# Causal linear attention and soft mixture on Trainium2: gamma times v summed on VectorE and carried by two passes with ones, and a new order in the last group

## The reference, cut to what matters

```python
# x: (4, 2048, 256)
h = lambda x, W1, b1: gelu(x @ W1 + b1)
q, k, v = (h(x, W1, b1) @ W2 + b2 for each of q, k, v)
scores = einsum('bid,bjd->bij', q, k) / sqrt(256 * 512)
out = einsum('bij,bjd->bid', scores * tril, v)           # no softmax
x = layernorm(x + (layernorm(out) * ln_w + ln_b))
xn = layernorm(x, ln_gamma, ln_beta)
logits = (unit(xn) * scale) @ unit(mu)                   # mu: 256 x 16 x 16
dispatch, combine = softmax(logits, tokens), softmax(logits, slots)
slot_in = einsum('bnd,bnes->besd', xn, dispatch)
h = gelu(slot_in @ w1 + b1);  slot_out = h @ w2 + b2
out = layernorm(x + einsum('besd,bnes->bnd', slot_out, combine))
```

## Time and profile before

| | us |
|---|---|
| median of 3 runs (lowest, highest) | 622.74 (622.67, 622.85) |
| profiled execution, its own time | 622.77 |
| its span (first to last instruction) | 621.0 |
| busy in the span: PE / PEld / DVE / ACT / POOL | 605.4 / 558.0 / 426.0 / 412.4 / 342.5 |

### The profile page before, as it was taken

One profiled execution on the slowest core, in us unless ns is written; L12 is line 12 of the kernel. 1 busy time (PEld: TensorE's weight loads), 2 busy tenths in 40 slices (PEclk: granted clock), 3 DMA queues, 4 the chain that ended last, 5 costly groups with the idle time before them and its releaser, 6 DMA issues. The chain is left out here.

```text
span 621.0 us, 12379 instructions
## 1 busy us (share of the span) xinstructions
PE 605.4 (97%) x4100; PEld 558.0 (90%) x4100; DVE 426.0 (69%) x948; ACT 412.4 (66%) x920; POOL 342.5 (55%) x359
## 2 busy tenths in 40 slices
PE   7999999999999999999999999989999999999995
PEld 5989989989999999999998999989999999988884
DVE  5377677677676776777777768897555556347876
ACT  4756767667677667776776776676766666535674
POOL 1737658568485585574855856766434433103443
PEclk9999999999999999999999999999999999999998
DMA  8301012012020210110201201020000000302444
GB/s 228 104 2 69 6 63 70 1 69 69 0 68 1 66 68 0 68 65 3 68 0 68 68 2 35 1 56 15 1 1 0 0 0 1 69 1 69 148 158 169
DMA packets 29326, 30.21 MB, mean 49 GB/s; under 512 B 5326, under 2 KB 25196, under 8 KB 29292
## 3 DMA queue, kind: packets, MB, share of 16 engines
q1 hardware_dynamic: 29280, 29.78, 15.0%
q10 hardware_dynamic: 12, 0.00, 0.0%
HBM read 21.39 MB, written 8.39 MB: 48 GB/s over the span
## 5 line engine op out<-in xcount | busy, mean ns | idle before, releaser
L488 POOL TENSOR_TENSOR h_lo<-xn_all,h_hi 128x512 fp32r<-128x512 f32 x32 | 41.4, 1294 | 126.1 <-ACT xn_all L565 126.0
L563 ACT ACTIVATE h_hi<-bank,bias_col 128x512 fp32r<-128x512 f32 x96 | 66.3, 691 | 35.2 <-PE bank L690 31.8
L1067 DVE TENSOR_TENSOR state_lo<-bank,state_hi 128x512 fp32r<-128x512 f32 x57 | 39.2, 688 | 60.9 <-ACT state_hi L604 60.9
L688 PE MATMUL bank<-xnT_hi,w_hi 128*128 128x512 f32 x188 | 76.1, 405 | 0.0
L690 PE MATMUL bank<-xnT_hi,w_lo 128*128 128x512 f32 x188 | 74.3, 395 | 0.0
L689 PE MATMUL bank<-xnT_lo,w_hi 128*128 128x512 f32 x188 | 74.3, 395 | 0.0
L1460 PE MATMUL bank<-xn_all,e_tok 128*128 128x257 f32 x256 | 66.4, 382 | 0.5 <-ACT slot_inT L1388 0.3
L1365 ACT ACTIVATE e_tok<-bank,shift,xinv 128x256 f32<-128x256 f32 x64 | 36.1, 564 | 45.0 <-PE bank L1443 24.8
L1540 DVE COPY ET_all<-bank 128x256 f32<-128x256 f32 (+1 forms) x64 | 27.0, 424 | 53.3 <-PE bank L1454 52.9
L604 ACT CAST state_hi<-bank 128x512 fp32r<-128x512 f32 x57 | 33.5, 587 | 39.2 <-PE bank L830 39.1
L1532 PE MATMUL bank<-w_sb,ET_all 128*128 128x256 f32 x256 | 55.4, 380 | 0.0
(11 more groups left out here) (192 smaller groups left out, 2080.7 us busy)
## 6 DMA issues: line engine op xcount, KB each, us to landing
x_all<-in_L_attn_x SPq DMA_DIRECT2D x16, 512.0 KB, 3.5
xn_all<-in_xT SPq DMA_DIRECT2D x15, 512.0 KB, 4.4
out<-xn_all SPq DMA_DIRECT2D x15, 512.0 KB, 3.0
w_sb<-in_L_ffn_w SPq DMA_DIRECT2D x2, 512.0 KB, 5.2
xn_all<-in_L_ffn_w SPq DMA_DIRECT2D x2, 512.0 KB, 6.2
xn_all<-in_xT SPq DMA_DIRECT2D x2, 256.0 KB, 3.6
out<-xn_all SPq DMA_DIRECT2D x2, 256.0 KB, 2.5
x_all<-in_L_attn_W2k SPq DMA_DIRECT2D x1, 258.0 KB, 4.4
```

The lines of the kernel that those rows point to most:

```text
L488: pool.tensor_tensor(h_lo[:, V_SLOT, m, :], hv[:, m, :], h_hi[:, V_SLOT, m, :].bitcast(F32), ALU.subtract).then_inc(hv_split, 1)
L563: nc.scalar.activation(h_hi[:, h_slot(j, n), m, :], ps, ACT.Gelu, bias=bias(n, m))
L688: nc.tensor.matmul(ps, w[0], xs[0], start=start, stop=False, skip_group_check=shared)
L1067: nc.vector.tensor_tensor(lo[:, :, :], state_halves, hi[:, :, :].bitcast(F32), ALU.subtract).then_inc(state_split, 1)
```

## The change

1. The gamma column times v is summed per token place (partition) on DVE: `sum_v` adds chunk after chunk into `v_sum`, which has four places for the four chunks of a group; `close_sum` hands the last one on to the next group. ACT rounds the sums in pairs (`round_vsum`), POOL subtracts for the low half (`split_vsum`). `carry` is now two passes per chunk, with ones as weights, inside the chunk that needs it, and nothing is copied between output tiles. `preload`, `mark_out`, `split_gamma`, `gam_hi` and `gam_lo` are gone.
2. `causal` is one 128x128 mask in place of four; `warm_up` runs three products of the size of `mark_out`'s two.
3. `sum_mu_squares` runs ahead of `project_v(0)` of group 0, and floor, inversion and factors move ahead with it.
4. In the last two bodies the orders of ACT, DVE and POOL are written anew.

```diff
+            v_sum = asb("v_sum", [P, GT, D])
+            vsum_hi = asb("vsum_hi", [P, GT, D], F32R)
+            vsum_lo = asb("vsum_lo", [P, GT, D], F32R)
+            ones_r = asb("ones_r", [P, P], F32R)
-            causal = asb("causal", [P, GT, P])
+            causal = asb("causal", [P, P])
...
 # POOL
+                def split_vsum(g, m):
+                    pool.wait_ge(vsum_rounded, 2 * g + m + 1)
+                    pair = slice(2 * m, 2 * m + 2)
+                    pool.tensor_tensor(vsum_lo[:, pair, :], v_sum[:, pair, :], vsum_hi[:, pair, :].bitcast(F32),
+                                       ALU.subtract).then_inc(vsum_split, 1)
                 def body(g, j, ba, attend=True, project=True, settle=True, more=True):
                     a = g - 1
                     if not project:
                         invert_norms(pool, 0, 0, minus_half[:, :])
+                        invert_z(pool, a - 1, j % 2)
+                        add_ln_b(a)
                         add_beta(pool, 1, 1)
                         invert_x1(pool, a - 1, j % 2)
                         return
+                    if attend and project:
+                        split_vsum(a, 0)
                     if project:
                         split_hv(g, 0)
                     if attend:
                         invert_o(pool, a, 0)
                     if project:
+                        if attend:
+                            split_vsum(a, 1)
                         split_hv(g, 1)
                         if more:
                             split_x(g + 1)
-                        add_ln_b(g)
-                        if not more:
+                        if not attend:
+                            invert_mu_norms()
+                        if more:
+                            add_ln_b(g)
+                        else:
                             add_beta(pool, 0, 0)
                         split_ktok(g, 0)
...
+                        if not more:
+                            split_vsum(g, 0)
+                            split_vsum(g, 1)
-                    if attend and project:
+                    if attend and project and more:
                         invert_z(pool, a, (j - 1) % 2)
-                        if more:
-                            invert_x1(pool, a, (j - 1) % 2)
+                        invert_x1(pool, a, (j - 1) % 2)
 # ACT
-                def preload(ba, i):
-                    act.wait_ge(carried, CB * ba + i - 1)
-                    act.wait_ge(z_ready, TB * ba + i + 2 - i % 2)
-                    nc.scalar.copy(out_tile(i % GT), out_tile((i - 1) % GT)).then_inc(preloaded, 1)
+                def round_vsum(g, m):
+                    act.wait_ge(v_summed, GT * g + 2 * m + 1)
+                    pair = slice(2 * m, 2 * m + 2)
+                    nc.scalar.copy(vsum_hi[:, pair, :], v_sum[:, pair, :]).then_inc(vsum_rounded, 1)
...
                         round_xnT(act, 0, 0)
+                        round_vsum(a, 0)
                         round_state(ba, i + 1, tail_hi[1])
-                        preload(ba, i + 2)
-                        nc.scalar.activation(warm[:, :], warm[:, :], ACT.Exp).then_inc(table_warm, 1)
+                        round_vsum(a, 1)
+                        apply_z(act, a - 2, ja % 2, (2, 3))
                         round_state(ba, i + 2, tail_hi[2])
                         round_masked(a)
-                        preload(ba, i + 3)
-                        apply_z(act, a - 1, (ja - 1) % 2, (0, 1))
                         round_state(ba, i + 3, tail_hi[3])
-                        apply_z(act, a - 1, (ja - 1) % 2, (2, 3))
+                        nc.scalar.activation(warm[:, :], warm[:, :], ACT.Exp).then_inc(table_warm, 1)
+                        apply_z(act, a - 1, (ja - 1) % 2, range(GT))
                         return
...
                     hidden(g, j, WK1, 0)
+                    if attend:
+                        round_vsum(a, 0)
...
                         follow(0)
+                    if attend:
+                        round_vsum(a, 1)
                     hidden(g, j, WV1, 0)
 # PE
-                def carry(a, ba, i):
-                    c = i % GT
...
-                    split3(out_tile((i + 1) % GT),
-                           (gam_hi[:, c:c + 1].to_broadcast([P, P]), gam_lo[:, c:c + 1].to_broadcast([P, P])),
-                           (v_hi[:, c, :], v_lo[:, c, :]), False, False, shared=True).then_inc(carried, 1)
+                def carry(a, c, start):
+                    pe.wait_ge(vsum_split, 2 * a + c // 2 + 1)
...
+                    nc.tensor.matmul(out_tile(c), ones_r[:, :], vsum_hi[:, c, :], start=start, stop=False,
+                                     skip_group_check=True)
+                    nc.tensor.matmul(out_tile(c), ones_r[:, :], vsum_lo[:, c, :], start=False, stop=False,
+                                     skip_group_check=True)
...
                     elif c == 0:
-                        read_state(ba, i, c, p, False)
+                        read_state(ba, i, c, p, True, False)
+                        carry(a, c, False)
                         last = attend_chunk(a, c, False, True)
                     else:
-                        attend_chunk(a, c, False, False)
-                        last = read_state(ba, i, c, p, True)
+                        attend_chunk(a, c, True, False)
+                        carry(a, c, False)
+                        last = read_state(ba, i, c, p, False, True)
                     last.then_inc(chunk_done, 1)
                     if i < TB - 1:
                         update_state(a, c, i == 0)
-                        carry(a, ba, i)
 # DVE
-                def split_gamma(g):
-                    dve.wait_ge(gam_rounded, g + 1)
-                    nc.vector.tensor_tensor(gam_lo[:, :], k_tok[:, :, D], gam_hi[:, :].bitcast(F32), ALU.subtract
-                                            ).then_inc(gam_split, 1)
+                def sum_v(g, j, c):
+                    dve.wait_ge(v_biased, 2 * g + c // 2 + 1)
...
+                    gamma = k_tok[:, c, D:D + 1]
+                    if j == 0 and c == 0:
+                        last = nc.vector.tensor_scalar(v_sum[:, 1, :], v_tok[:, 0, :], gamma, None, ALU.mult)
+                    else:
+                        last = nc.vector.scalar_tensor_tensor(out=v_sum[:, c + 1, :], in0=v_tok[:, c, :], scalar=gamma,
+                                                              in1=v_sum[:, c, :], op0=ALU.mult, op1=ALU.add)
...
                         split_masked(a)
...
+                    if attend:
+                        sum_v(a, ja, 1)
+                        sum_v(a, ja, 2)
                     split_h(g, j, WQ1, 0)
...
                         follow(0)
+                        close_sum(a, ja)
                     split_h(g, j, WQ1, 1)
...
                     bias_v(g, j, 1)
+                    if not more:
+                        for c in range(GT - 1):
+                            sum_v(g, j, c)
+                        return
                     if attend:
                         add_out(dve, a, 2)
                         add_out(dve, a, 3)
                         z_summed(dve, a, 1)
-                    split_gamma(g)
+                    sum_v(g, j, 0)
...
                     floor_norms(dve, 0, 0)
                     tail_state(1)
+                    add_out(dve, a - 1, 2)
+                    add_out(dve, a - 1, 3)
                     mask_scores(a)
-                    shift_z(dve, a - 1, 1 - p)
                     tail_state(2)
                     split_masked(a)
+                    z_summed(dve, a - 1, 1)
+                    z_statistics(a - 1, 1 - p, 1)
+                    tail_state(3)
                     split_xnT(dve, 0, 0)
-                    tail_state(3)
+                    z_deviation(dve, a - 1, 1 - p)
+                    dve.wait_ge(v_split, 2 * GROUPS)
                     scale_tokens(2, 2)
+                    shift_z(dve, a - 1, 1 - p)
```

More of the change, by code:

```diff
@@ L663, in body @@
                         follow(2)
-                        if settle:
+                        if settle and more:
                             apply_z(act, a - 1, (ja - 1) % 2, range(GT))
+                        if not more:
+                            norms(act, 0, 0, range(GT))
                         follow(3)
@@ L752, in fold_weights, with warm_up @@
                     last.then_inc(ku_done, 1)
[L754 to L759 removed]
+                def warm_up():
+                    for ps in (*out_ps, state_ps):
+                        nc.tensor.matmul(ps[:, :], ident[:, :], causal[:, :].unsqueeze(1).to_broadcast([P, GT, P]),
+                                         start=True, stop=True)
                 def project_k(g, j, t):
@@ L1188, in _ @@
                 split_weight(WV2)
+                nc.vector.tensor_copy(ones_r[:, :], ones[:, :]).then_inc(ones_rounded, 1)
                 body(0, 0, 0, attend=False)
```

(1 more changed line is left out.)

87 lines of the change are left out of this document (44 added, 43 removed).

## The result

The changed kernel takes 630.12 us (median of 4 runs, 629.85 to 631.76), the kernel before 622.80 (4 runs, 622.67 to 623.61): 1.012 times as long, 95% interval 1.0101 to 1.014. The forecast was 630.4, slower. The profiled execution took 629.85 us with a span of 628.1, 7.1 more than the one before (622.77 and 621.0). The sum is right; several of its terms are not, and their errors cancel.

The account below looks back on a forecast made before the run. PE, busy 97% of the span, was taken to bound the kernel. Terms +0.5 - 1.5 - 5.9 + 4.0 + 8.6 + 1.9 = +7.6 us on 622.77 gave 630.4 us, range 624.5 to 636.

Parts of the forecast that it names:

- The last group, +8.6: Block end: late ve_z, then 7.7 us of GpSimd work, moves the end from 414.3 to 422.9, +8.6 us.
- The clock, +1.9: Routing stage: after PE idles some 8 us it begins at the low clock, +1.9 us (0 to 2.3).
- The carry, -5.9: Carries up to the last projecting body's second chunk: two passes (0.24 us) replace three (0.34 us), -5.9 us.
- The wait at chunk 0, +4.0: Chunk 0's carry in 11 groups: PE waits 0.36 us each for the split sums, +4.0 us.
- rival 1: The sums fit in: no wait at chunk 0, DVE not held in the last group; 624.8, up to 627; chance 0.17.
- mu's norms, -1.5: Group 0: factors ready long before the scores end, so PE's wait for them goes, -1.5 us.
- The one wait named in the price: Group 0, chunk 0: a possible wait for the unit mu, giving back at most 1.5 us.
- The start, +0.5: Kernel start: smaller mask starts PE 0.7 us earlier, two more warm_up passes cost time; net +0.5 us (-0.2 to +1.0).

Follow-up runs that it names:

- k1_pool: The changed kernel with add_ln_b and add_beta moved ahead of invert_z in GpSimd's queue of the last group; 626.61 us, 1.0064 of before.
- k5_nosum: The changed kernel with the sums, their rounding and split on 2 columns instead of 256, the carry reading v_hi and v_lo; 626.5 us, 1.005 of before.
- k2_warm: The changed kernel with 30 more 512-column passes on PE behind the last pass of the last group; 629.82 us, 1.0102 of before.
- b1_carry6: The kernel before with the three passes of each carry done twice; 643.89 us, 1.0329 of before.
- k6_carry4: The changed kernel with the two passes of each carry done twice; 641.99 us, 1.0297 of before.
- b2_wide: The kernel before with the carry's weights taken from plain 128x128 tiles of ktok_hi and ktok_lo instead of one repeated gamma column; 624.82 us, 1.003 of before.
- k7_delay: The changed kernel with a pow of about 1.0 us ahead of GpSimd's split_vsum(a,0) in each group; 638.91 us, 1.0252 of before.
- k3_biasv: The changed kernel with mu_factors on DVE behind bias_v(1) of the first group instead of ahead of it; 631.49 us, 1.0138 of before.
- k10_acttail: k8_hybrid with ACT's roundings ahead of its four L188, sum 2 behind the first tail state, three warm_up products, mu_factors as in the change; 621.77 us, 0.9979 of before.
- k8_hybrid: The changed kernel with group 14's z_deviation and invert_z early, ln_b(15) in halves, two warm_up products, mu_factors behind bias_v(1); 621.30 us, 0.9967 of before.

## Why the prediction was right, point by point

- **The last group, +8.6: right, +8.1.** Its mechanism is shown by k1_pool (the place of two additions in GpSimd's queue, at least 2.65 us at the mark and 3.5 in the time) and k5_nosum (1.35 of the 1.6 for the sums held by GpSimd). `ve_z` came at 411.5; the 415.2 of the forecast, less the 3.3 us by which the last scores start earlier, are 411.9. The 7.7 us of work were 7.8. The Trainium skill, "SBUF — State Buffer", section "Who interferes with whom", says that a DVE instruction with two inputs in SBUF contends with a GpSimd instruction that reads SBUF; the traces agree: 1.52 us instead of 0.49 for a sum, 3.77 instead of 1.67 for the four L212.
- **The clock, +1.9: right, +2.2** (the rest in k2_warm against the changed kernel). That the sizes are so near is partly luck: 1.9 was half of 3.7 us, taken from the kernel's start, and the low level lasted 5.5 us into the routing stage.
- **The carry, -5.9: the size failed, -3.3.** The step "0.34 us for three passes, 0.12 each for two" priced the passes rightly (b1_carry6, k6_carry4; the sum used 0.236 for two, which with 0.24 is -5.6) and assumed that every other pass keeps its spacing. The 53 carries in "groups" give -5.3. The v projection behind them takes back 0.8, of which 0.5 is shown to go with the repeated column (b2_wide, in the kernel before); the k projection takes back 0.9, cause open; waits in the last projecting body and small differences 0.3. The 0.5 of k5_nosum doesn't come on top: most of it lies in the carries and in the passes that read the state, which are nearly as short in k6_carry4 with all sums in place.
- **The wait at chunk 0, +4.0: failed, 0.** It was a difference of 0.36 us between two long lines. Set on one scale (the last update's pass at 298.72 before, 296.36 after, so +2.36), the split ends at 310.53 instead of 310.8: `v_lo` was held by 0.18 us, not 0.36 (2.71 for 2.53). And PE wants the sums at 310.68 instead of 310.59, as its passes are further apart. k7_delay shows that the line is as tight as I thought; I had its sign wrong. The 0.1 us for the restart, of which nothing was shown, is 0.06 there. This was rival 1's first half; its second half (DVE not held in the last group) did not happen.
- **mu's norms, -1.5: failed.** The step "the factors are then ready long before the scores end" was right. What I left out is who stands behind them on DVE: `bias_v(1)`, and through ACT the copy that frees the scores' bank. The one wait named in the price was another one.
- **The start, +0.5**: 0.0 in this profile, but up to +1.0 in others, see below. Start and mu's norms together are 0.0 where -1.0 was forecast.
- Two errors of about the same size, a stall of 4.0 that did not come and a gain of 5.9 and 1.0 that came as 3.3 and 0, cancel in the sum: that 630.4 is so near 630.1 is luck. The verdict did not hang on them: the last group and its clock alone are +10.4.

## What to carry to other kernels

In a queue written out by hand, put what is ready early ahead of what waits for another engine: two additions, 4.9 us of work that could have begun in a 4.1 us gap, stood behind one wait and cost 2.65 us or more at the block's end. When a piece of work is moved into another engine's gap, list who stands behind it there (here `bias_v(1)`), and whether a DVE instruction with two inputs in SBUF comes to stand beside a GpSimd instruction that reads SBUF: in these traces such pairs ran one behind the other (0.49 us became 1.2 to 1.5), so the time of one can't hide behind the other. When several changes meet in one time, cut the trace at marks common to both kernels and compare the parts; the sum alone would have called this prediction sound in every step, and k2_warm a clock that costs nothing.

## What the runs showed of the hardware that was not expected

- **A repeated column as weights goes with a closer spacing.** The carry's three passes take 0.343 us with it and 0.359 with a plain tile, and the twelve passes of the v projection behind it are 0.114 us apart from start to start, not 0.118 (b2_wide). Behind the other carries of a group nothing changes. Together 1.3 us for 53 carries.
- **The same passes can cost more in another build.** The k projection's passes are 0.120 us apart in the kernel before and 0.1225 in the changed one, 0.9 us in "groups"; the cause is open.
- **The pace of the first passes is not the same in every execution.** Six passes of `warm_up` take 4.38 to 5.49 us, and PE goes on at 6.63 to 7.73. PE's next instruction in the changed kernel and in k3_biasv:

```profile
6.70 0.22 PE L916 MATMUL bank<-ident,bias_rows 6*128 6x6 f32 x1
```

```profile
7.73 0.27 PE L916 MATMUL bank<-ident,bias_rows 6*128 6x6 f32 x1
```

  The passes are 0.85 us apart until some moment between 5.4 and past 6.7, then 0.43. The profile's windows show a granted clock of 1.00 all that time, but the trace's table of the clock has no entry at all before 5.60 us in the changed kernel, 8.04 in k3_biasv and 11.77 in b1_carry6, and the spacing halves where the table begins (in b1_carry6 passes of 512 columns go from 0.43 to 0.23 us apart at 11.78). So the 1.00 ahead of it says nothing, and my text, which called this stretch the low clock, took that from the spacing alone. Of the ten profiles with three products PE goes on before 7 us in four, at 7.19 and 7.35 in two, at 7.72 or 7.73 in four; "start" is 56.6 to 56.8 where it is late, and 55.4 to 56.2 where it is not (k10_acttail, 7.19, among these; the 56.83 of k6_carry4, 7.35, has 0.45 of doubled passes in it). The 59.77 of b1_carry6 is four doubled carries, 1.4 us, and the latest rise of all. With two products (k8_hybrid) PE goes on at 6.02, but the slow pace then lasts into the first hidden layer.
- **At the end of the block a wait of 1.3 us of PE cost no clock, one of 3.6 us cost all of it.** "Rest" takes 206.0 where PE was idle for 0.5 to 1.3 us ahead of it, 208.1 after 3.63, 207.1 to 208.2 after 7.3 to 7.8.
